# A vision tower's attention: scores and maxima two steps ahead, stacks by group of heads, patches split in other steps

## The chip, the core and the metric

The kernel runs on one core of one Trainium2 chip. The metric is the device time of one execution in microseconds. A core has five engines that run their own instruction streams and meet at semaphores: TensorE (PE in the rows, its weight loads PEld), VectorE (DVE), ScalarE (ACT), GpSimd (POOL) and SyncE (SP), which issues the DMA transfers here.

## The reference

64 images of 224 x 224 go through a patch projection, one attention layer with a residual, and one expert layer with a residual. Cut to what matters:

```python
h = patches(x) @ W.T + b                         # 64 x 196 tokens x 192
xn = layernorm(layernorm(h)) * g + beta          # token-wise, twice
q, k, v = split(xn @ qkv_w.T + qkv_b)            # 12 heads of 16
attn = q @ k.T * 16 ** -0.5                      # 196 x 196 for each head
attn = attn - 0.2 * sum_of_8_neighbours(attn)    # 3 x 3 window, centre left out
attn = softmax(attn - max(attn))
h = h + attn @ v
n = layernorm(h)
score = relu(n @ Wr1.T + br1) @ Wr2.T + br2      # 8 experts, the best 2, softmax weights
h = h + sum over the 2 experts of w_e * (relu(n @ W1[e].T + b1[e]) @ W2[e].T + b2[e])
```

## The kernel before

Two phases follow each other. The change touches the first, the attention phase; the second, the expert phase (router, then 56 tiles of 512 rows), is left as it is.

The attention phase works on pairs of images: 32 pairs, each of four half-image tiles of 98 tokens. A pair has six **steps**: 2 images x 3 groups of 4 heads. A step number within a pair is called k = 0 to 5 here (`kk % STEPS` in the code; `kk` runs over the 12 steps of a body, which is two pairs). The order is written out by hand: each engine has a function `step(body, kk)`, and `run_bodies` (line 137) calls it for a filling, for bodies 0 and 1 written out, for the other bodies in a hardware loop, and for the last body with a drain. Nothing is reordered: an engine that waits in its stream holds all that stands behind it.

What a pair goes through:

1. SyncE loads the patches (`x_buf`, two buffers). ScalarE casts each tile to a 16-bit high part (`high_patches`), GpSimd subtracts to get the low part (`split_patches`), TensorE projects (`project_patches`, 18 matmuls for a tile), VectorE adds the bias (`take_h`) and takes `statistics`; SyncE stores h.
2. GpSimd takes the inverse deviation (`var_eps`, `rstd`) and normalises (`layernorm`, tile `xn`); TensorE transposes (`transpose_xn`); VectorE and ScalarE take the results (`take_xt_a`, `take_xt_b`) and split them into high and low parts (`split_high`, `split_low`).
3. TensorE projects queries and keys in three blocks (`project_qk`); ScalarE evicts them to `padded` (`take_qk`). GpSimd adds the two neighbours (`add_beside`), VectorE adds the centre (`add_tilde`). ScalarE rounds both versions to 16 bits (`take_high_plain`, `take_high_tilde`), VectorE takes what rounding left (`take_low_plain`, `take_low_tilde`). SyncE stores these to DRAM (`store_parts`) and reads them back in stacks of 96 rows (`stack`): one matmul over a stack gives a score with the neighbours already subtracted. Before, 6 transfers of 12 heads each bring a pair's stacks.
4. TensorE projects values (`project_v`); VectorE evicts them (`take_v`).
5. The attention itself, once a step. `scores` (tile `s_bank`, two banks, one for even and one for odd heads) are only for the row maxima (`row_maxima`, `split_maxima` on VectorE). The maxima are transposed (`transpose_max`, into `m_bank`) and copied by ScalarE as extra rows of the query stack (`copy_max_rows`). `scores_less_max` (tile `t_bank`) computes the scores again, transposed, with the maxima subtracted by the matmul. ScalarE takes `exponentials` to `probs`, TensorE multiplies with the values (`mix`), ScalarE copies (`copy_mixed`), TensorE transposes back into `m_bank` (`transpose_back`), VectorE divides (`normalise`).
6. GpSimd adds h (`sum_rows`), VectorE takes statistics (`statistics_n`), GpSimd and ScalarE normalise, split the rows (`high_rows`, `low_rows`) and SyncE stores them for the experts.

In step s TensorE works on the scores of s + 1, the transposed scores of s, the mix of s - 1 and the transposing back of s - 2. The projections of the next pairs lie between, in the functions `before_max` and `after_max`: before and behind the transpose of the maxima. `m_bank` is shared by the transposed maxima and the transposing back, and so `transpose_back` waits for ScalarE's copy of the max rows. In every second pair ScalarE, VectorE and GpSimd also convert a part of the expert weights (`high_part`, `low_part`); in body 0 at kk = 3 SyncE issues the transfers that blank the memory of the expert slots (`blank_memory`).

Of the kernel before, what the change touches and what calls it, by code (L numbers as in the profile page):

```python
# [47 lines left out]
DRAIN = STEPS + 1  # L48
# [88 lines left out]
def run_bodies(eng, step):  # L137

    step(0, -1)
    for body in range(2):  # L140
        for kk in range(BODY_STEPS):
            step(body, kk)
    with eng.Fori(2, BODIES - 1) as body:
        for kk in range(BODY_STEPS):
            step(body, kk)
    for kk in range(BODY_STEPS + DRAIN):
        step(BODIES - 1, kk)


def attention_phase(nc, x_t, w_tok, w_qk_a, w_qk_b, w_v_a, w_v_b, b_tok, b_qk, b_v, ln_cols, row_consts, ident_in,  # L150
# [4 lines left out]
    with ctx:  # L155
# [130 lines left out]
        q_stacked = sem("q_stacked")  # L286
        k_stacked = sem("k_stacked")
# [60 lines left out]
        def patch_uses(u, b):  # L348

            return 1 if isinstance(u, int) and u == 0 else USES[b] * u  # L350
# [10 lines left out]
        def _(sp):  # L361
# [95 lines left out]
            def step(body, kk):  # L457
                k = kk % STEPS
                if kk == -1:
# [5 lines left out]
                    store_h(Pair(0, 0, 0))  # L465
                    for low in range(2):
                        store_parts(Pair(0, 0, 0), low)
                    for low in range(2):
                        stack(Pair(0, 0, 0), low)
                    store_h(Pair(0, 0, 1))  # L470
                elif k == 0:
                    load_x(Pair(body, kk, 2))
                    load_h(Pair(body, kk, -1))
                    store_rows(Pair(body, kk, -2))
                elif k == 1:
                    if kk == 1 and not (isinstance(body, int) and body == 0):
                        store_part(body - 1)
                    elif kk == BODY_STEPS + 1:
                        store_part(body)
                    for low in range(2):  # L480
                        store_parts(Pair(body, kk, 1), low)
                    for low in range(2):
                        stack(Pair(body, kk, 1), low)
                elif k == 3:
                    store_y(Pair(body, kk, -1))
                elif k == 4:
                    store_h(Pair(body, kk, 2))
                if kk == 3 and isinstance(body, int) and body == 0:
# [17 lines left out]
        def _(pe):  # L506
            pe.wait_ge(wtok_split, 2)

            def project_patches(pr, half, c):

                if pr.there:
                    if c == 0:
                        wait(pe, padded_ready, BLOCKS * (pr.u - 1) + (3, 2)[half])
# [4 lines left out]
                    for f in range(PCH):  # L518
# [28 lines left out]
            def project_qk(pr, i):  # L547

                if pr.there:
                    if i == 0:  # L550
                        pe.wait_ge(x_split, 4 * (pr.u + 1))
                    bank, ready = claim(pr, 2 + i)
                    out = bank[:, 0:COLS]
# [6 lines left out]
            def project_v(pr, im, tiles):  # L560

                if pr.there and tiles[0] == 0:
# [3 lines left out]
                    else:  # L566
                        pe.wait_ge(h_ready, 2 * (pr.u + 1) + im + 1)
# [1428 lines left out]
```

## Time and profile before

| | |
|---|---|
| median of three runs | 2195.34 us (2183.92, 2195.34, 2195.45) |
| the profiled execution | 2189.16 us, span 2187.4 us |
| busy share of the span | TensorE 86%, VectorE 67%, ScalarE 58%, GpSimd 53% |
| DMA | 382.56 MB, 175 GB/s on average |
| granted TensorE clock | 0.925 of full speed on average |

The span runs from the first to the last instruction of the profiled execution. Busy shares of a whole span are averages over stages with different limits: the attention phase ends at about 1232 us, and VectorE is busy in it to a much higher share than in the expert phase. In the rows, the bracket at the end of a line gives the idle time of the engine just before the instruction, and what ended it. "issue" stands where the profile names nothing that was waited for.

### The profile page before, as it was taken

How to read it: one execution, taken by the hardware profiler on the slowest of the kernel's cores; microseconds unless marked ns; L12 is line 12 of the kernel's file. 1: busy time of each engine (PE TensorE's matmuls, PEld its weight loads, DVE VectorE, ACT ScalarE, POOL GpSimd, SP SyncE). 2: the span in 40 equal slices, each digit the busy share in tenths (PEclk: the TensorE clock that was granted, in tenths of full speed). 3: DMA queues.
4: the chain of work that ended last, by engine and by line, in shares of the span. 5: the costliest groups of instructions: out<-in, count | busy, mean ns of one | idle time of the engine just before them, and what ended most of it. 6: DMA issues, size and time to landing. Idle time of an engine off the chain costs nothing. (4 is left out here: it accounts for less than half of the span.)

```text
span 2187.4 us, 54001 instructions
## 1 busy us (share of the span) xinstructions
PE 1891.2 (86%) x17949; PEld 1406.2 (64%) x17949; DVE 1461.1 (67%) x4652; ACT 1266.8 (58%) x2469; POOL 1152.0 (53%) x1069
## 2 busy tenths in 40 slices
PE   4758888888888989898888479999999999999991
PEld 3546666666666666666665256777777777777771
DVE  4658888888888888888887345655555555554440
ACT  3557788787878788787877323433434343333330
POOL 3335555555555545555552254666666666654452
PEclk7878999999999999999999559999999999999996
DMA  4564746666574747575664237787877878798876
GB/s 142 144 187 143 202 147 190 168 182 168 173 197 146 215 142 198 161 195 157 183 173 132 65 106 197 186 211 184 206 185 205 190 201 194 190 195 184 180 176 193
DMA packets 356572, 382.56 MB, mean 175 GB/s; under 512 B 138388, under 2 KB 319952, under 8 KB 352144
## 3 DMA queue, kind: packets, MB, share of 16 engines
q1 hardware_dynamic: 314768, 338.64, 55.3%
q0 software_dynamic: 41664, 42.12, 11.1%
q8 instruction: 80, 1.31, 0.2%
q14 instruction: 60, 0.49, 0.1%
HBM read 232.83 MB, written 135.46 MB: 168 GB/s over the span
## 5 line engine op out<-in xcount | busy, mean ns | idle before, releaser
L1838 ACT ACTIVATE mh<-mid_bank 128x512 bf16<-128x512 f32 x336 | 200.8, 598 | 464.0 <-PE mid_bank L1529 349.6
L824 DVE TENSOR_REDUCE row_max<-s_bank 98x2 f32<-98x392 f32 x768 | 396.6, 558 | 97.6 <-PE s_bank L607 94.7
L1750 DVE SCALAR_TENSOR_TENSOR ml<-mid_bank,mh 128x512 bf16<-128x512 f32 x336 | 231.6, 689 | 341.9 <-ACT mh L1838 333.7
L1020 ACT ACTIVATE probs<-t_bank 98x392 f32<-98x392 f32 x768 | 340.6, 498 | 42.1 <-PE t_bank L623 31.1
L1904 POOL DMA_INDIRECT sums<-y_out,tail x168 | 265.1, 1578 | 172.9 <-DVE y_out L1780 95.8
L1543 PE MATMUL y_bank<-wst,mh 128*128 128x192 bf16 x1344 | 330.0, 246 | 8.3 <-DVE y_out L1780 7.5
L1546 PE MATMUL y_bank<-wst,ml 128*128 128x192 bf16 x1344 | 330.1, 246 | 0.0
L1545 PE MATMUL y_bank<-wst,mh 128*128 128x192 bf16 x1344 | 329.8, 245 | 0.0
L623 PE MATMUL t_bank<-q_stack,k_stack 104*98 104x196 f16 x1536 | 248.6, 269 | 40.0 <-ACT probs L1020 25.5
L1193 POOL TENSOR_TENSOR x_lo<-x_buf,x_hi 128x588 f16<-128x588 f32 x128 | 188.7, 1478 | 170.6 <-ACT x_hi L1001 112.8
L1889 POOL DMA_INDIRECT slots<-row_r,spot x196 | 190.7, 973 | 98.0 <-issue 56.7
L623 PEld LDWEIGHTS t_bank<-q_stack,k_stack 104*98 104x98 f16 x1536 | 152.5, 130 | 112.3 <-ACT probs L1020 108.6
L519 PE MATMUL p_bank<-wtok_h,x_hi 128*98 128x192 f16 x768 | 201.7, 263 | 18.2 <-POOL x_lo L1193 18.2
L607 PE MATMUL s_bank<-k_stack,q_stack 96*98 96x196 f16 x1536 | 204.0, 256 | 6.1 <-DVE row_max L824 5.3
L520 PE MATMUL p_bank<-wtok_l,x_hi 128*98 128x192 f16 x768 | 199.7, 260 | 0.0
L521 PE MATMUL p_bank<-wtok_h,x_lo 128*98 128x192 f16 x768 | 198.7, 259 | 0.0
L1037 ACT COPY q_stack<-m_bank 8x784 f16<-8x784 f16 x192 | 154.4, 804 | 66.5 <-PE m_bank L647 63.5
L636 PE MATMUL o_bank<-probs,v_buf 98*32 98x196 f32 x3072 | 171.5, 341 | 18.1 <-ACT probs L1020 18.0
L1201 POOL TENSOR_TENSOR beside<-padded 128x1176 f32<-128x1176 f32 x32 | 68.7, 2146 | 195.3 <-ACT padded L1064 195.3
L607 PEld LDWEIGHTS s_bank<-k_stack,q_stack 96*98 96x98 f16 x1536 | 153.2, 130 | 12.7 <-DVE row_max L824 7.4
L1543 PEld LDWEIGHTS y_bank<-wst,mh 128*128 128x128 bf16 x1344 | 134.3, 100 | 41.1 <-issue 19.5
L1545 PEld LDWEIGHTS y_bank<-wst,mh 128*128 128x128 bf16 x1344 | 131.0, 97 | 19.6
(236 smaller groups left out, 4515.7 us busy)
## 6 DMA issues: line engine op xcount, KB each, us to landing
wst<-packed SPq DMA_DIRECT2D x56, 1584.0 KB
x_buf<-in_x_t SPq DMA_DIRECT2D x32, 1176.0 KB, 9.0
q_stack<-stack_parts SPq DMA_DIRECT2D x96, 294.0 KB, 4.8
k_stack<-stack_parts SPq DMA_DIRECT2D x96, 294.0 KB, 6.7
stack_parts<-qk_hi SPq DMA_DIRECT2D x32, 588.0 KB, 2.9
stack_parts<-qk_lo SPq DMA_DIRECT2D x32, 588.0 KB, 2.8
sums<-h_buf SPq DMA_DIRECT2D x32, 294.0 KB
h_in<-sums SPq DMA_DIRECT2D x32, 294.0 KB
```

Of the source, the lines that this page charges most:

```text
L519: nc.tensor.matmul(out, x_hi[:, f, tokens], wtok_h[:, f, :], start=(f == 0), stop=False)
L520: nc.tensor.matmul(out, x_hi[:, f, tokens], wtok_l[:, f, :], start=False, stop=False)
L607: last = nc.tensor.matmul(s_bank[hh % 2][0:HALF, u, 0:TOKENS], q_stack[st.q][0:PARTS, head, head_cols(st, u)], k_stack[st.q][0:PARTS, head ...
L623: last = nc.tensor.matmul(out, k_stack[st.q][:, head, head_cols(st, v)], q_stack[st.q][:, head, head_cols(st)], start=True, stop=True)
L824: nc.vector.reduce_max(row_max[st.odd][:, :, hh:hh + 1], s_bank[hh % 2][0:HALF, :, 0:TOKENS], AX.X).then_inc(max_ready, 1)
L1020: nc.scalar.activation(probs[st.odd][:, hh], t_bank[hh % 2][0:HALF, :, 0:TOKENS], ACT.Exp).then_inc(probs_ready, 1)
L1543: nc.tensor.matmul(o, mh[n % MID][:, cols], high, start=(c == 0 and j % 2 == 0), stop=False, skip_group_check=True)
L1545: nc.tensor.matmul(o, mh[n % MID][:, cols], low, start=False, stop=False, skip_group_check=True)
L1546: last = nc.tensor.matmul(o, ml[n % MID][:, cols], high, start=False, stop=False, skip_group_check=True)
L1750: nc.vector.scalar_tensor_tensor(ml[n % MID][:], mid_bank[n % MID_PS][:], 0.0, mh[n % MID][:], ALU.max, ALU.subtract).then_inc(ml_ready, 1)
L1838: nc.scalar.activation(mh[n % MID][:], mid_bank[n % MID_PS][:], ACT.Relu).then_inc(mh_ready, 1)
L1904: nc.gpsimd.indirect_dma_start(out=total_rows, out_offset=bass.IndirectOffsetOnAxis(ap=to, axis=0), in_=y_out[q][:, j, :], in_offset=None, ...
```

## The change

- TensorE's `scores` and VectorE's `row_maxima` and `split_maxima` work two steps ahead (`LOOK = 2`), not one; `transpose_max` and `copy_max_rows` stay one step ahead. The filling is four calls of `step` instead of one, the drain is longer by four steps.
- `stack` takes a group of heads: 18 transfers a pair of a third of the size, with semaphores of their own for each group; `scores` waits at the first step of each group of image 0. SyncE issues them in k = 2 and 3, and the patches are loaded three pairs ahead instead of two.
- TensorE's other work is put into `between_heads` (before the last two heads of the second scores) and `after_heads` (behind the transposed maxima): patches in k = 0, 1, 2 instead of 1 and 2, both value projections in k = 3, both transposes of xn at the end of k = 4, query/key behind everything in k = 5.
- VectorE: the second `take_h` in k = 3, both `statistics` at the end of k = 3, both `take_v` in k = 4.
- ScalarE: one patch cast in each of k = 0, 2, 4, 5 (for two or three pairs ahead); `copy_max_rows` directly behind the exponentials; the rows of the second layernorm a pair later.
- GpSimd: one split of patches in each of k = 0, 3, 4, 5, none in k = 1, where it waits for `take_low_plain`.
- The filling interleaves the first two pairs.

```diff
-DRAIN = STEPS + 1
+DRAIN = 2 * STEPS - 1
+LOOK = 2
+FILL = 4
...
-            def stack(pr, low):
+            def stack(pr, low, g):
...
-                        sp.dma_start((q_stack, k_stack)[which][pr.q][32 * r:32 * r + 32], src
-                                     ).then_inc((q_stacked, k_stacked)[which], 16)
+                        sp.dma_start((q_stack, k_stack)[which][pr.q][32 * r:32 * r + 32, HG * g:HG * (g + 1)],
+                                     src[:, :, g]).then_inc((q_stacked, k_stacked)[which][g], 16)
...
                 elif k == 0:
-                    load_x(Pair(body, kk, 2))
+                    load_x(Pair(body, kk, 3))
...
-            def before_max(body, kk):
+            def between_heads(body, kk):
 
                 k = kk % STEPS
-                if k in (1, 2):
-                    project_patches(Pair(body, kk, 2), k - 1, 0)
+                if k in (0, 1):
+                    project_patches(Pair(body, kk, 2), 0, k)
+                elif k == 2:
+                    project_patches(Pair(body, kk, 2), 1, 0, range(PCH // 2, PCH))
                 elif k == 3:
                     project_v(Pair(body, kk, 1), 0, (0, 1))
+
+            def after_heads(body, kk):
+
+                k = kk % STEPS
+                if k == 1:
+                    project_patches(Pair(body, kk, 2), 1, 0, range(PCH // 2))
+                elif k == 2:
+                    project_patches(Pair(body, kk, 2), 1, 1)
+                elif k == 3:
+                    project_v(Pair(body, kk, 1), 1, (0, 1))
                 elif k == 4:
...
                     transpose_xn(Pair(body, kk, 2), 0)
...
                     transpose_xn(Pair(body, kk, 2), 1)
                 elif k == 5:
-                    project_qk(Pair(body, kk, 2), 2)
+                    for i in range(BLOCKS):
+                        project_qk(Pair(body, kk, 2), i)
...
             def step(body, kk):
-                if kk == -1:
+                if kk == -FILL:
                     fill_pipeline()
-                scores(Step(body, kk, 1), (0, 1))
+                scores(Step(body, kk, LOOK), (0, 1))
                 mix(Step(body, kk, -1))
                 transpose_back(Step(body, kk, -2))
                 scores_less_max(Step(body, kk, 0), (0, 1))
-                scores(Step(body, kk, 1), (2, 3))
+                scores(Step(body, kk, LOOK), (2, 3))
+                if kk >= 0:
+                    between_heads(body, kk)
                 scores_less_max(Step(body, kk, 0), (2, 3))
-                if kk >= 0:
-                    before_max(body, kk)
                 transpose_max(Step(body, kk, 1))
                 if kk >= 0:
-                    after_max(body, kk)
+                    after_heads(body, kk)
...
                     elif k == 2:
+                        statistics_n(Pair(body, kk, -1))
+                    elif k == 3:
                         statistics(Pair(body, kk, 2), 0)
-                        statistics_n(Pair(body, kk, -1))
-                        take_h(Pair(body, kk, 2), 1)
-                    elif k == 3:
-                        take_v(Pair(body, kk, 1), 0)
+                        statistics(Pair(body, kk, 2), 1)
```

The order of VectorE around k = 3, first before the change: `h_buf` is the second half of h, `row_max` and `max_parts` the maxima and their split, `stats` and `meanvar` the statistics that GpSimd waits for.

```order
L864 SCALAR_TENSOR_TENSOR h_buf<-p_bank,btok 98x384
L824 TENSOR_REDUCE row_max<-s_bank 98x2 x2
L847 RECIPROCAL recip<-m_bank 98x8
L851 TENSOR_TENSOR att<-m_bank,recip 98x2x64
L872 BN_STATS stats<-h_buf 98x6 x2
L877 MEMSET spacer 98x1
L879 BN_AGGR meanvar<-stats 98x2 x4
L824 TENSOR_REDUCE row_max<-s_bank 98x2 x2
L832 TENSOR_SCALAR max_parts<-row_max 98x2x4
L835 SCALAR_TENSOR_TENSOR max_parts<-row_max,max_parts 98x2x4
L902 TENSOR_TENSOR v_buf<-p_bank,bv 98x24x16
```

And after the change, the same step:

```order
L896 SCALAR_TENSOR_TENSOR h_buf<-p_bank,btok 98x384
L856 TENSOR_REDUCE row_max<-s_bank 98x2 x2
L864 TENSOR_SCALAR max_parts<-row_max 98x2x4
L867 SCALAR_TENSOR_TENSOR max_parts<-row_max,max_parts 98x2x4
L904 BN_STATS stats<-h_buf 98x6 x4
L909 MEMSET spacer 98x1
L911 BN_AGGR meanvar<-stats 98x2 x4
L856 TENSOR_REDUCE row_max<-s_bank 98x2 x2
L879 RECIPROCAL recip<-m_bank 98x8
L883 TENSOR_TENSOR att<-m_bank,recip 98x2x64
L934 TENSOR_TENSOR v_buf<-p_bank,bv 98x24x16 x2
```

The statistics stood ahead of the maxima of heads 2 and 3; now they stand behind them and their split, and values are evicted one step later.

TensorE at the end of k = 4, first before the change (`t_bank` second scores, `s_bank` scores for maxima, `wv` the value projection, `ident,xn` the transposes of xn):

```order
L623 MATMUL t_bank<-q_stack,k_stack 98x196 x4
L607 MATMUL s_bank<-k_stack,q_stack 98x196 x4
L623 MATMUL t_bank<-q_stack,k_stack 98x196 x4
L573 MATMUL p_bank<-wv_ah,x_ah 98x192
L574 MATMUL p_bank<-wv_al,x_ah 98x192
L575 MATMUL p_bank<-wv_ah,x_al 98x192
L576 MATMUL p_bank<-wv_bh,x_b 98x192
L577 MATMUL p_bank<-wv_bl,x_b 98x192
L543 MATMUL p_bank<-ident,xn 128x98 x4
L647 MATMUL m_bank<-ident,max_parts 128x98 x2
L543 MATMUL p_bank<-ident,xn 128x98 x4
```

And after the change, from the transposing back of k = 4 on:

```order
L616 MATMUL m_bank<-ident,mixed 98x128 x2
L650 MATMUL t_bank<-q_stack,k_stack 98x196 x4
L634 MATMUL s_bank<-k_stack,q_stack 98x196 x4
L650 MATMUL t_bank<-q_stack,k_stack 98x196 x4
L674 MATMUL m_bank<-ident,max_parts 128x98 x2
L566 MATMUL p_bank<-ident,xn 128x98 x8
L634 MATMUL s_bank<-k_stack,q_stack 98x196 x4
```

The value projection has left the step, and the eight transposes of xn stand directly behind the transposed maxima, with nothing else between them and the next step's scores.

GpSimd from `beside` (k = 0) to the second layernorm's deviation (k = 2), before the change:

```order
L1201 TENSOR_TENSOR beside<-padded 128x1176
L1193 TENSOR_TENSOR x_lo<-x_buf,x_hi 128x6x98 x4
L1208 TENSOR_TENSOR att<-att,h_in 98x768
L1213 TENSOR_TENSOR var_n<-meanvar_n,eps_n 98x4
L1216 TENSOR_TENSOR rstd_n<-var_n,minus_half 98x4
```

And after the change, from the splits of k = 4 and 5 on:

```order
L1227 TENSOR_TENSOR x_lo<-x_buf,x_hi 128x6x98 x2
L1235 TENSOR_TENSOR beside<-padded 128x1176
L1227 TENSOR_TENSOR x_lo<-x_buf,x_hi 128x6x98
L1242 TENSOR_TENSOR att<-att,h_in 98x768
L1247 TENSOR_TENSOR var_n<-meanvar_n,eps_n 98x4
L1250 TENSOR_TENSOR rstd_n<-var_n,minus_half 98x4
```

One split (`x_lo`) is left behind `beside`; the others went to k = 3, 4 and 5.

## Rows read from the trace of the kernel before

**Rows 1.** Windows: busy us (instructions) by engine, clock, DMA share, GB/s.
```profile
128.50:1161.00 1032.50, 909.48 (x9559) 680.34 (x9560) 870.37 (x2244) 824.95 (x1590) 542.34 (x536) 0.95 0.62 174
```

**Rows 2.** Timeline, GpSimd: start us, us, instruction [idle before, releaser]; once a pair.
```profile
438.15 0.20 POOL L1166 TENSOR_TENSOR var_eps<-meanvar,one_eps 98x4 f32<-98x4 f32 x1 [1.27 <-DVE meanvar L879]
...
473.60 0.20 POOL L1166 TENSOR_TENSOR var_eps<-meanvar,one_eps 98x4 f32<-98x4 f32 x1 [1.00 <-DVE meanvar L879]
...
507.92 0.20 POOL L1166 TENSOR_TENSOR var_eps<-meanvar,one_eps 98x4 f32<-98x4 f32 x1 [1.28 <-DVE meanvar L879]
...
545.00 0.20 POOL L1166 TENSOR_TENSOR var_eps<-meanvar,one_eps 98x4 f32<-98x4 f32 x1 [1.03 <-DVE meanvar L879]
...
616.35 0.20 POOL L1166 TENSOR_TENSOR var_eps<-meanvar,one_eps 98x4 f32<-98x4 f32 x1 [1.00 <-DVE meanvar L879]
...
650.66 0.20 POOL L1166 TENSOR_TENSOR var_eps<-meanvar,one_eps 98x4 f32<-98x4 f32 x1 [1.28 <-DVE meanvar L879]
...
721.43 0.20 POOL L1166 TENSOR_TENSOR var_eps<-meanvar,one_eps 98x4 f32<-98x4 f32 x1 [1.27 <-DVE meanvar L879]
```

**Rows 3.** Waits, 200 to 1050 us: total us, times, longest us.
```profile
DVE row_max L824 <- PE s_bank L607: 65.6, 84, 3.5
...
PE m_bank L647 <- DVE max_parts L835: 43.1, 61, 1.0
...
PE m_bank L589 <- issue: 17.5, 24, 1.0
```

**Rows 4.** Timeline, 619 to 652 us: GpSimd, TensorE, VectorE.
```profile
619.53 2.18 POOL L1183 TENSOR_TENSOR xn<-centred,rstd 98x512 f32<-98x512 f32 x3 [0.17 <-POOL centred L1177]
...
628.94 0.50 PE L607 MATMUL s_bank<-k_stack,q_stack 96*98 96x196 f16 x4
...
639.69 1.44 DVE L931 SCALAR_TENSOR_TENSOR qk_lo<-tilde,tilde_scale,qk_hi 128x1176 f16<-128x1176 f32 x1
...
641.71 1.04 DVE L824 TENSOR_REDUCE row_max<-s_bank 98x2 f32<-98x392 f32 x2 [0.57 <-PE s_bank L607]
...
643.03 0.21 DVE L847 RECIPROCAL recip<-m_bank 98x8 f32<-98x8 f32 x1 [0.28 <-PE m_bank L589]
...
647.61 0.56 DVE L864 SCALAR_TENSOR_TENSOR h_buf<-p_bank,btok 98x384 f32<-98x384 f32 x1 [0.16 <-PE p_bank L521]
...
650.50 1.01 DVE L824 TENSOR_REDUCE row_max<-s_bank 98x2 f32<-98x392 f32 x2
...
651.75 0.17 DVE L835 SCALAR_TENSOR_TENSOR max_parts<-row_max,max_parts 98x8 f16<-98x8 f32 x1
```

**Rows 5.** Source line 921: count, duration ns min/median/max.
```profile
L921 DVE TENSOR_TENSOR qk_lo<-padded,qk_hi x32: 1373/2224/2295, 39.3 to 1167.9; 128x1176 f16<-128x1176 f32 x32
```

**Rows 6.** Windows around falls of the clock, and the router stage.
```profile
666.90:670.40 3.50, 2.02 (x26) 1.02 (x25) 3.41 (x7) 3.45 (x7) 1.69 (x2) 0.93 0.11 42
670.40:677.20 6.80, 6.76 (x45) 6.77 (x46) 5.61 (x9) 5.43 (x10) 4.00 (x3) 0.53 0.22 89
...
520.20:523.60 3.40, 3.40 (x16) 1.86 (x14) 1.13 (x3) 2.27 (x4) 0.00 (x0) 0.57 0.34 127
...
1240.00:1320.00 80.00, 53.01 (x298) 38.87 (x299) 31.16 (x232) 18.69 (x43) 36.36 (x45) 0.50 0.38 118
```

**Rows 7.** SyncE's queue: stack transfers in the timeline, and size, us to landing.
```profile
607.94 1.30 SPq L384 DMA_DIRECT2D q_stack<-stack_parts  x2
...
k_stack<-stack_parts SPq DMA_DIRECT2D x90, 294.0 KB, 6.7
```

**Rows 8.** Timeline of the fill (TensorE, SyncE, ScalarE); groups of the tail, 1161 to 1222.
```profile
73.19 0.89 PE L623 MATMUL t_bank<-q_stack,k_stack 104*98 104x196 f16 x4 [0.56 <-ACT q_stack L1037]
...
117.90 0.43 SPq L366 DMA_DIRECT2D x_buf<-in_x_t  x1
...
127.00 0.68 ACT L1001 CAST x_hi<-x_buf 128x588 f16<-128x588 f32 x1 [17.62 <-DMA x_buf<-in_x_t]
...
L647 PE MATMUL m_bank<-ident,max_parts 98*128 98x98 f16 x22 | 3.0, 218 | 7.1 <-DVE max_parts L835 7.0
```

More of the change, by code:

```diff
@@ L137, in run_bodies @@
 def run_bodies(eng, step):
-    step(0, -1)
+    for kk in range(-FILL, 0):
+        step(0, kk)
     for body in range(2):
@@ L142, in run_bodies @@
             step(body, kk)
-    with eng.Fori(2, BODIES - 1) as body:
+    with eng.Fori(2, BODIES - 2) as body:
         for kk in range(BODY_STEPS):
             step(body, kk)
+    for kk in range(BODY_STEPS):
+        step(BODIES - 2, kk)
     for kk in range(BODY_STEPS + DRAIN):
@@ L599, in scores @@
                 if st.there:
-                    if st.first and heads[0] == 0:
-                        pe.wait_ge(q_stacked, (st.pair + 1) * STACKED)
-                        pe.wait_ge(k_stacked, (st.pair + 1) * STACKED)
+                    if st.image == 0 and heads[0] == 0:
+                        pe.wait_ge(q_stacked[st.group], (st.pair + 1) * STACKED)
+                        pe.wait_ge(k_stacked[st.group], (st.pair + 1) * STACKED)
                     for hh in heads:
@@ new lines, in fill_pipeline @@
+                pe.wait_ge(weights_in, 16 * len(LOADS))
+                pe.wait_ge(consts_set, CONSTS)
+                transpose_xn(first, 0)
+                transpose_xn(first, 1)
+                for c in range(2):
+                    project_patches(second, 0, c)
+                for i in range(BLOCKS):
+                    project_qk(first, i)
+                for c in range(2):
+                    project_patches(second, 1, c)
+                project_v(first, 0, (0, 1))
+                project_v(first, 1, (0, 1))
@@ L936, in fill_pipeline @@
                 first, second = Pair(0, 0, 0), Pair(0, 0, 1)
[L937 to L949 removed]
+                for half in range(2):
+                    take_h(first, half)
+                    statistics(first, half)
+                take_xt_a(first)
+                split_low(first)
+                for half in range(2):
+                    take_h(second, half)
+                    statistics(second, half)
+                add_tilde(first)
+                take_v(first, 0)
+                take_v(first, 1)
+                take_low_plain(first)
+                take_low_tilde(first)
+                take_xt_a(second)
+                split_low(second)
                 set_up_rows()
@@ L1007, in _ @@
             for i in range(2):
+                if i == 1:
+                    for tile in range(TILES):
+                        high_patches(Pair(0, 0, 1), tile)
                 for hh in range(HG):
@@ L1113, in fill_pipeline @@
                     pr = Pair(0, 0, u)
-                    if u == 1:
-                        for tile in range(TILES):
-                            high_patches(pr, tile)
                     take_xt_b(pr)
@@ L1126, in step @@
                 k = kk % STEPS
-                if kk == -1:
+                if kk == -FILL:
                     fill_pipeline()
```

187 lines of the change are left out of this document (91 added, 96 removed).

## The prediction

> **What bounds the kernel now.** I read the stretches first. The steady part of the attention, 1032.5 us, is half of the span; there TensorE is busy 88%, VectorE 84%, ScalarE 80%, GpSimd 53% [rows 1]. No engine is full, so what sets a pair's time is a chain of waits. Second, the pair's period from one instruction that occurs once a pair [rows 2]: 438.15 to 721.43 is 283.3 us for 8 pairs, 35.4 each. An undisturbed pair takes 34.3 (473.60 to 507.92), the one whose steps also convert expert weights 35.5 (438.15 to 473.60), and the one from 507.92 to 545.00 takes 37.1, though of the second kind. Third, the waits [rows 3], for 24 pairs: TensorE stands 43.1 us before the transpose of the maxima and 17.5 before transposing back (nothing named; by the code it waits there for ScalarE's copy of the max rows). That is 2.5 us a pair, and what the change aims at. But VectorE waits 65.6 for scores too, so two engines hand the delay to each other.
>
> The chain of an undisturbed pair, 616.35 to 650.66: GpSimd normalises until xn is ready at 619.53 + 2.18 = 621.71 (5.4 us); TensorE transposes it at once, then query/key, "beside", tilde and the split of the low parts until 639.69 + 1.44 = 641.13 (19.4 us); from there VectorE takes h and its statistics until GpSimd starts at 650.66 (9.5 us, 1.0 of it waits: 0.57, 0.28, 0.16) [rows 2, 4]. Sum 34.3, the measured period. So the loop xn to xn sets the pair, and each edit is priced by what it does to this loop.
>
> **The change, part by part, in the steady state.** (1) Maxima one step earlier: the transpose of the maxima no longer waits, and ScalarE copies the max rows before its other work, not behind it. Both waits go, 2.5 us a pair on TensorE. TensorE was not the loop, though: behind k = 0 and 1 what is late next is VectorE's own row of work (tilde, low plain, two pairs of maxima, low tilde). I value it at nothing beyond the waits of VectorE it removes, counted in (3).
> (2) GpSimd's splits of patches leave step k = 1, where they lay beside VectorE's "low plain" subtraction. That takes 2.22 us in the median but 1.37 at its fastest [rows 5], which is the one that no split overlaps. After the change GpSimd waits for it. It is on the loop: -0.85 us. The Trainium skill (SBUF — State Buffer, "Who interferes with whom") says that a VectorE instruction with two SBUF inputs and a GpSimd one exclude each other; the trace agrees with 2.22 against 1.37, and the value above is the row's.
> (3) Statistics of both halves move behind the maxima of heads 2 and 3 in k = 3. Before, these maxima and their split followed the statistics (650.50 to 651.75 + 0.17, 1.4 us [rows 4]); now they stand ahead of them on VectorE. The 1.0 us of waits in the stretch goes, since TensorE is now a step ahead. Net +0.4 us.
> (4) ScalarE in k = 5: a patch cast (0.68) before the last two exponentials, and the three query/key evictions behind the max rows. The third projection needs the bank of the first, so it waits for that eviction. Worked through with the durations before, k = 5 ends 7.3 us behind xn against 7.2 (621.71 to 628.94 [rows 4]): +0.1; in the odd pair the weight cast makes it +0.7, which before cost 1.2.
> Steady sum without the clock: -0.35 even, about -0.9 odd, mean -0.65 us a pair. Over 29 pairs: -19 us. Bounds: nothing of it (0) to all 2.5 us of TensorE's waits (-73); I stay at the loop.
>
> (5) The new wait. TensorE's xn transposes now stand behind the whole of k = 4, with both value projections already gone to k = 3. Scores of heads 2 and 3 in k = 4 need VectorE's next maxima (1.04 us behind the statistics), so TensorE is through about 1.7 us behind the statistics, and xn comes 5.4 behind them: 3.7 us idle in every pair, where it waited under 0.2. This time is in the loop already. What it does to the clock is not. TensorE's granted clock falls to the lower level (1.2 of 2.4 GHz) after 666.90 to 670.40, in which it waited for 1.5 of 3.5 us; in the router stage, where it idles for a third of 80 us, it stays at 0.50 throughout [rows 6]. The new wait is longer in one piece than what went before the fall at 670.40, so I expect a fall in nearly every pair, covering 3 to 4 us of the transposes, k = 5's scores, mix and back. There TensorE is on the loop: the mix would end at 3.8 instead of 2.2 us behind xn and push ScalarE's exponentials by 1.1 to 1.4. The row of before with a fall at such a place: 507.92 to 545.00 took 37.1, 1.6 over its like, with 0.57 granted at 520.20 [rows 2, 6]; falls with patches beside them cost nothing. Falls cost 35.4 - 34.9 = 0.5 a pair now. I take 1.15 after: +0.6 net, 29 pairs, +17 us. Bounds: 0 granted loss (-16) and 1.6 plus a second stretch, 2.4 a pair (+55).
> The Trainium skill (TensorE: Matmul & The Clock Gate, "HAM oscillation — how this bites in real kernels") says that a kernel whose matmuls come in bursts with waits between is slowed anew after every wait. The rows on the router stage agree; it speaks against this change, and without it the sum would be 17 us lower.
>
> (6) SyncE: 18 stack transfers a pair for 6, same bytes. Issue of one took 0.65 us (two in 1.30 [rows 7]); at that price 3.9 us for the six of group 0, 11.7 in all, of a 35 us period. Median to landing 6.7 us [rows 7]. Group 0 is needed at k = 4 now, not k = 5: low tilde ends at 18.6 in the loop, + 1.1 for the store, + 3.9, + 6.7 = 30.3; TensorE wants it at about 27.5, a microsecond before the statistics end; since xn comes at 33.9 (34.3 - 0.35) and a step's own scores, mix and transposes take about 3, it can take it up to 30.9. Hidden, barely: 0, other end in the rivals. Moved row stores and h stores have whole steps of slack.
>
> **One-time parts.** Fill: the first second-scores start at 73.2 [rows 8]. The second pair's patches, casts and statistics now run inside the first pair's waits. Walking it with the old durations: low tilde of pair 0 is ready 3.3 us later (the second pair's h, statistics and values stand before it), but xn of pair 1 and with it the end of its query/key projections, at about 55, comes 13.4 earlier, group 0's stack lands about then; one more step of scores and maxima is run first. First second-scores at about 60.7: -12.5 (bounds -4 to -16).
> Stall: at 109 ScalarE stands 17.6 us for pair 3's patches, whose load SyncE issues only at 117.9, behind the blank stores, and which lands 9 us later [rows 8]. After the change that load goes out at step 0; the first load behind the blanks is pair 4's, needed two steps later (about 109 in the new frame), issued at 106 to 112: 6 to 12 us of stall remain, and pair 2's stack queues behind it. -7 (bounds 0 to -17.6).
> Tail: the last two pairs have light steps, with 7.0 us of waits of TensorE for the maxima in them [rows 8]; the last pair's rows come 4 steps later but these are empty, except that pair 30's low rows (1.65 us) now stand before pair 31's. -6 + 2 = -4.
>
> **Sum.** -12.5 - 7 - 4 - 19 + 17 = -25.5. The profiled execution took 2189.16 (span 2187.4 + 1.76); it gives 2163.7. The median of the runs shown is 6.2 higher, 2195.34, which would give 2169.8; the three runs lie 11.5 apart, so I take the middle, 2167.
>
> **Rivals.**
> A, the clock does not fall more than now: the 17 us are not paid, 2167 - 17 = 2150. For it: most falls of before lie beside patches and cost nothing; against: the router stage, and the place of this one. With the waits of (1) gaining more than the loop says, down to 2125. Chance 0.25.
> B, no change: falls last twice as long, or cost 1.6 to 2 us a pair, which is +0.85 x 29 = +25: 2192. For it: the 6.8 us stretch at 670.40 [rows 6]. Chance 0.17.
> C, slower: the stack becomes the loop. Group 0's six transfers with the twelve others right behind land later than 30.9 us. Each microsecond beyond costs one a pair; it decides from 0.9 us beyond (25.5 / 29). At 2 us beyond, + 58 - 25.5: about 2225. For it: the 0.6 us of slack above, 9 us landings of patches in the same queue; against: group 0 is a third of the bytes, and is issued first. Chance 0.12.
> D, the edit does not do what it says: TensorE goes on waiting for maxima, since the score banks still allow only two heads ahead, and the loop stays 35.4, with only the one-time parts gained: -23.5, 2169; the same side and nearly the number of my forecast. It shows as waits for row maxima before scores. Chance 0.11.
> Forecast, 0.35: 2167, own range 2148 to 2186.
>
> Faster or slower by under 0.5% (11 us, 2184.4 to 2206.3) is what a measurement cannot tell from no change. Faster: nearly all of A and D, 0.9 of the forecast, 0.15 of B: 0.68. Same: 0.7 of B, 0.1 of the forecast, a fifth of C: 0.18. Slower: the rest, 0.14. The range holds the forecast, most of A, all of B: 2130 to 2204.
>
> **What would show it.** Period of the var_eps instruction: 35.2 even with the clock's loss, 33.9 without (A), over 36 (B, C). TensorE idle 3 to 4 us before the xn transposes each pair, waiting for GpSimd's xn; granted clock of the steady part under 0.95, and below 0.7 right behind that wait. Low plain at 1.4 us. No wait before the transpose of the maxima. C: a wait before the first-step scores for DMA of the stacks. First second-scores at 58 to 66 us. A stall for patches under 12 us near 115. If the transposes don't wait, (5) is wrong, and if low plain stays 2.2, so is (2).

## The result, and the profile after

The changed kernel takes 2277.75 us (median of 4, 2276.83 to 2284.16) against 2194.03 (2183.92 to 2195.45) before: ratio 1.039, 95% interval 1.0375 to 1.0413. It is 84 us slower. The forecast of 2167 and its range failed, and so did the sign.

The span grew from 2187.4 to 2282.1 us, by 94.7. The instruction that occurs once a pair, GpSimd's first on the variance (`var_eps`), splits this into three parts. First its line in both traces (count, min/median/max ns, first and last start), after and then before:

```profile
L1200 POOL TENSOR_TENSOR var_eps<-meanvar,one_eps x32: 200/200/1249, 21.4 to 1235.5; 98x4 f32<-98x4 f32 x32
```
```profile
L1166 POOL TENSOR_TENSOR var_eps<-meanvar,one_eps x32: 198/199/201, 20.0 to 1145.9; 98x4 f32<-98x4 f32 x32
```

Up to the fifth of them the change is ahead: it starts at 179.70 against 184.05, -4.4 us. The 27 periods from there to the last take 39.10 instead of 35.63 us: +94.0. From the last to the end it is 1046.6 against 1041.5: +5.1, which comes from the expert phase, where the program is the same. The loss is the steady pair. The steady stretch of after (columns as in [rows 1]: TensorE matmul, its weight loads, VectorE, ScalarE, GpSimd, clock, DMA share, GB/s):

```profile
130.00:1240.00 1110.00, 916.65 (x9334) 722.63 (x9334) 914.12 (x2214) 809.31 (x1556) 511.53 (x529) 0.85 0.51 159
```

The granted clock is 0.85 where it was 0.95 [rows 1]. VectorE, which was meant to lose waits, has grown in work: 914 us for about the same instructions. Where it grew is in its groups, 200 to 1050 us (busy us, mean ns, idle before): before, then after.

```profile
L832 DVE TENSOR_SCALAR max_parts<-row_max 98x8 f16<-98x8 f32 x143 | 32.2, 225 | 5.0
L835 DVE SCALAR_TENSOR_TENSOR max_parts<-row_max,max_parts 98x8 f16<-98x8 f32 x143 | 24.4, 171 | 4.9
```
```profile
L864 DVE TENSOR_SCALAR max_parts<-row_max 98x8 f16<-98x8 f32 x131 | 89.7, 685 | 5.5
L867 DVE SCALAR_TENSOR_TENSOR max_parts<-row_max,max_parts 98x8 f16<-98x8 f32 x131 | 52.4, 400 | 4.5
```

Two instructions on 98 x 8 numbers went from 0.40 to 1.09 us together, six times a pair: 4.1 us a pair. The timeline of after shows how (start us, us, instruction, [idle before, releaser]), at about the time of [rows 4] (the pair before that one): first k = 4, then k = 1, GpSimd and VectorE.

```profile
615.85 2.18 POOL L1217 TENSOR_TENSOR xn<-centred,rstd 98x512 f32<-98x512 f32 x3 [0.17 <-POOL centred L1211]
```
```profile
615.87 1.62 DVE L864 TENSOR_SCALAR max_parts<-row_max 98x8 f16<-98x8 f32 x1
617.53 0.53 DVE L867 SCALAR_TENSOR_TENSOR max_parts<-row_max,max_parts 98x8 f16<-98x8 f32 x1
...
634.80 1.38 DVE L953 TENSOR_TENSOR qk_lo<-padded,qk_hi 128x1176 f16<-128x1176 f32 x1 [0.44 <-ACT qk_hi L1111]
...
637.16 1.11 DVE L864 TENSOR_SCALAR max_parts<-row_max 98x8 f16<-98x8 f32 x1
```
```profile
636.42 1.83 POOL L1242 TENSOR_TENSOR att<-att,h_in 98x768 f32<-98x768 f32 x1 [2.35 <-DVE qk_lo L953]
```

The split of the maxima ends with GpSimd's instruction: 617.53 + 0.53 = 618.06 against 618.03, and 637.16 + 1.11 = 638.27 against 638.25. So it was held until GpSimd was through, inside its own duration, and no view of waits lists this. Unhindered the two take 0.34 us, 0.17 each. The low plain is down to 1.38 us from 2.2 [rows 5], as forecast; the 0.44 us ahead of it, a wait for ScalarE's rounding, is new.

The waits of after, 200 to 1050 us, that answer to [rows 3]:

```profile
PE p_bank L566 <- POOL xn L1217: 69.3, 22, 3.8
PE s_bank L634 <- DVE row_max L856: 49.1, 33, 1.9
DVE row_max L856 <- PE s_bank L634: 44.9, 51, 2.7
DVE xt_a L917 <- PE p_bank L566: 23.0, 22, 1.6
```

TensorE no longer waits ahead of the transpose of the maxima, but 3.15 us a pair for xn, and 2.2 for row maxima ahead of scores, of which the kernel before has none. Behind the first its clock is down (windows of TensorE: busy, clock, DMA share, GB/s):

```profile
615.40:618.80 3.40, 0.78 (x7) 0.78 0.92 315
618.80:622.20 3.40, 3.40 (x29) 0.50 0.47 136
622.20:625.60 3.40, 3.40 (x24) 0.71 0.00 0
```

For what follows I cut each pair's loop in four, means over the 21 to 25 pairs from 200 to 1080 us, from the timelines of the marks that the prediction used (var_eps, end of xn, start of "beside", end of low tilde); the last column is the mean granted clock in the 4 us that begin 5.4 us behind var_eps, where TensorE starts on xn.

| kernel | var_eps to xn | xn to beside | beside to low tilde | low tilde to var_eps | pair | clock |
|---|---|---|---|---|---|---|
| before | 5.35 | 9.62 | 10.78 | 9.66 | 35.41 | 1.00 |
| after | 5.36 | 10.62 | 11.79 | 11.29 | 39.07 | 0.50 |
| e1 filler | 5.36 | 8.93 | 11.79 | 11.36 | 37.44 | 0.99 |
| e2 sum late | 5.36 | 10.55 | 10.86 | 11.17 | 37.94 | 0.50 |
| e3 stats early | 5.36 | 10.38 | 11.80 | 10.09 | 37.62 | 0.56 |
| e6 patches first | 5.36 | 10.60 | 11.80 | 11.16 | 38.92 | 0.50 |
| e7 (on before) | 5.36 | 9.71 | 11.19 | 9.68 | 35.94 | 1.00 |
| e8 three undone | 5.36 | 10.19 | 10.86 | 10.10 | 36.52 | 0.57 |
| e9 GpSimd order | 5.37 | 9.22 | 10.86 | 8.73 | 34.17 | 0.98 |
| e12 stats, GpSimd order | 5.37 | 10.12 | 11.80 | 8.43 | 35.72 | 0.83 |
| e13 GpSimd order alone | 5.36 | 10.90 | 11.80 | 9.50 | 37.55 | 0.50 |
| e14 (on before) | 5.35 | 10.21 | 10.64 | 11.25 | 37.45 | 0.75 |

The loss has three places: 1.0 behind xn, 1.0 around k = 1, 1.6 on the way to the next var_eps.

Not every microsecond by which VectorE's small instructions grew is on the loop. The six splits of the maxima of a pair take 2.4 us together before, 6.5 in the change, 8.2 in e13 and 4.7 in e9, from the same timelines, and e13 is faster than the change, e9 faster than before. What a collision costs depends on its place.

### The profile page after: what moved, and what is told of

It reads as the page before. It is cut to its first block and busy times, and to the rows that moved or that the text cites. A ratio compares the mean times of both kernels' runs of the same rounds, so it can differ in the third digit from the quotient of the medians.

```text
span 2282.1 us, 54318 instructions
## 1 busy us (share of the span) xinstructions
PE 1925.5 (84%) x17949; PEld 1469.8 (64%) x17949; DVE 1518.4 (67%) x4652; ACT 1270.8 (56%) x2469; POOL 1131.2 (50%) x1069
## 5 line engine op out<-in xcount | busy, mean ns | idle before, releaser
L634 PE MATMUL s_bank<-k_stack,q_stack 96*98 96x196 f16 x1536 | 240.1, 275 | 86.0 <-DVE row_max L856 78.6
L1227 POOL TENSOR_TENSOR x_lo<-x_buf,x_hi 128x588 f16<-128x588 f32 x128 | 167.8, 1314 | 238.1 <-ACT x_hi L1036 174.4
L634 PEld LDWEIGHTS s_bank<-k_stack,q_stack 96*98 96x98 f16 x1536 | 163.3, 138 | 123.7 <-DVE row_max L856 117.6
L650 PE MATMUL t_bank<-q_stack,k_stack 104*98 104x196 f16 x1536 | 229.5, 275 | 14.9 <-ACT probs L1058 13.7
L663 PE MATMUL o_bank<-probs,v_buf 98*32 98x196 f32 x3072 | 191.4, 372 | 16.6 <-ACT probs L1058 15.8
L650 PEld LDWEIGHTS t_bank<-q_stack,k_stack 104*98 104x98 f16 x1536 | 174.8, 140 | 27.8 <-ACT probs L1058 26.1
L566 PE MATMUL p_bank<-ident,xn 98*128 98x98 f32 x256 | 49.4, 373 | 108.5 <-POOL xn L1217 108.5
```

What stands on the lines that cost most here:

```text
L634: last = nc.tensor.matmul(s_bank[hh % 2][0:HALF, u, 0:TOKENS], q_stack[st.q][0:PARTS, head, head_cols(st, u)], k_stack[st.q][0:PARTS, head ...
L650: last = nc.tensor.matmul(out, k_stack[st.q][:, head, head_cols(st, v)], q_stack[st.q][:, head, head_cols(st)], start=True, stop=True)
```

## The experiments

Each was timed together with the kernel before, whose median was 2189 to 2191 us (2194 with the change), so differences to the change of under 5 us tell nothing. Ratios are to the kernel before; the changed kernel's is 1.039.

**e1, filler behind the wait.**
```diff
                     if n == 0:
+                        bank, ready = claim(pr, n)
+                        for _ in range((30 if not isinstance(pr.u, int) or pr.u > 1 else 0)):
+                            nc.tensor.matmul(bank[0:HALF, 0:DIM], x_ah[:, 0:HALF], wv_ah[:], start=True, stop=True)
                         pe.wait_ge(xn_ready, pr.u + 1)
                     bank, ready = claim(pr, n)
```


> The changed kernel with 30 more matmuls of 192 columns (results overwritten) put where TensorE waits for xn at the end of k = 4; they fill about 2.4 of the 3.1 us of the wait and change nothing else. Theory 1 (the clock: the wait for xn makes the granted clock fall over k = 5, and that costs what the loop lost): the low stretch behind the wait goes, xn to end of k = 5 falls from 9.4 back to about 7.3 us, period from 39.1 to about 37, median about 2278 - 2.1 x 27 = 2221. Theory 2 (GpSimd now lies over VectorE's small splits of the maxima, which take 0.69 and 0.40 us in the mean instead of 0.23 and 0.17): period stays within 0.3 of 39.1, median 2270 to 2286.


Measured: 2240.53, ratio 1.0225 (1.0201 to 1.0248). Only "xn to beside" moved, by -1.69 us, with the clock from 0.50 to 0.99. Work that computes nothing makes the kernel 37 us faster: the clock's share is real, 1.6 us a pair, and less than half of the loss.

**e2, row sum behind the low tilde.**
```diff
-                        pool.wait_ge(plain_lo_ready, Pair(body, kk, 1).u + 1)
+                        pool.wait_ge(tilde_lo_ready, Pair(body, kk, 1).u + 1)
                     sum_rows(Pair(body, kk, -1))
```


> The changed kernel, but GpSimd's row sum in k = 1 starts behind VectorE's split of the low tilde and no longer behind the low plain, so that it does not lie over the split of the maxima in k = 1. Theory 2 (port): that split falls from 1.1 to 0.2 us, it is on the loop, period -0.9, median about 2278 - 24 = 2254. Theory 1 (clock only): the 0.9 us is given back as a wait of VectorE or TensorE further on, median 2272 to 2284.


Measured: 2247.90, ratio 1.0251 (1.0228 to 1.0273), -30 us. "Beside to low tilde" fell by 0.93, what the split of the maxima had lost there. It is then as long as before the change, 10.86 against 10.78, although the low plain is 0.8 shorter: VectorE now has two waits in it that the kernel before has not (e2, 200 to 1050 us; total, times, longest):
```profile
DVE qk_lo L953 <- ACT qk_hi L1111: 11.5, 23, 0.6
DVE qk_lo L963 <- issue: 6.4, 23, 0.6
```

**e3, statistics early.**
```diff
                     elif k == 3:
-                        take_h(Pair(body, kk, 2), 1)
+                        statistics(Pair(body, kk, 2), 1)
...
                     elif k == 2:
+                        statistics(Pair(body, kk, 2), 0)
                         statistics_n(Pair(body, kk, -1))
-                    elif k == 3:
-                        statistics(Pair(body, kk, 2), 0)
-                        statistics(Pair(body, kk, 2), 1)
+                        take_h(Pair(body, kk, 2), 1)
```


> The changed kernel with VectorE's take of h and its statistics where they stood before (first half's statistics and the take of the second half at the end of k = 2, second statistics between the maxima of k = 3). Theory 3 (the order sets it: statistics behind the maxima make xn late): xn about 1.4 us earlier, TensorE's wait for it about 1.7 instead of 3.1 us, and if the clock then keeps up another 2: period about 35.7 to 37.7, median 2186 to 2240. Theory 2 (port): the split in k = 4 no longer lies under the normalising, but k = 3's does; period within 0.5 of 39.1 less the 0.3 of order, median 2262 to 2278.


Measured: 2239.65, ratio 1.0225 (1.0199 to 1.0252), -38 us; the wait for xn 1.9 us a pair, the clock still at 0.56. The part of the order came, that of the clock did not.

**e4, one step ahead** (`LOOK = 1`).


> The changed kernel with scores and maxima one step ahead instead of two, all else as changed. Theory A (looking two steps ahead is harmless, the loss is in the other moves): TensorE waits again for the maxima (2 us a pair, not on the loop), median 2268 to 2290. Theory B (two steps ahead itself is the loss: TensorE waits 2.2 us a pair for row maxima before scores of heads 2 and 3, and the fall of the clock in k = 2 comes from it): the wait and the fall in k = 2 go, period 37 to 38, median 2220 to 2250.


Measured: 2391.86, ratio 1.0912 (1.0888 to 1.0937): 114 us slower than the change. Both theories missed. TensorE then waits 180.9 us in 100 transposes of the maxima (200 to 1050 us). Looking two steps ahead is a gain in this order, not the loss.

**e5, value projections apart** (the second image's second tile back in k = 4, VectorE's takes back at the ends of k = 3 and 4).


> The changed kernel with the value projections as before: first image and the first tile of the second in k = 3, its second tile in k = 4, and VectorE takes them at the ends of k = 3 and k = 4. Theory 1 (clock): TensorE has 10 matmuls (0.8 us) and its own pace in k = 4, the wait for xn shrinks from 3.1 to about 2.3 us, the fall stays or goes at random: median 2240 to 2278. Theory 2 (port): VectorE's split of the maxima in k = 4 comes 0.5 us earlier but still under the normalising; nothing on the loop, median 2270 to 2286.


Measured: 2281.81, ratio 1.0428 (1.0395 to 1.0461): as the change. In this order, where TensorE waits for xn anyway, the place of the values costs nothing.

**e6, patches ahead of the scores in k = 2.**
```diff
+                if kk % STEPS == 2 and kk >= 0:
+                    between_heads(body, kk)
                 scores(Step(body, kk, LOOK), (2, 3))
-                if kk >= 0:
+                if kk % STEPS != 2 and kk >= 0:
```


> The changed kernel with, in k = 2 only, the patches that stood behind the scores of heads 2 and 3 put ahead of them, so that TensorE has work while VectorE takes the maxima of heads 0 and 1. If the second fall of the clock (in k = 2, behind waits of 1.6 and 0.8 us for row maxima) is on the loop: it goes or shortens, the later waits of VectorE for scores and of ScalarE for probabilities' input too, period -1 to -1.5, median 2238 to 2250. If it is not: the scores come later for VectorE by the patches' 1.5 us and the period stays or grows, median 2275 to 2310.


Measured: 2273.73, ratio 1.0380 (1.0347 to 1.0414): within 4 us. The fall in k = 2 did go (clock from 12 to 8 us ahead of var_eps: 0.86 in the change, 1.00 here), and so did VectorE's 1.14 us wait for scores in k = 3. VectorE came earlier and met GpSimd (e6, VectorE and then GpSimd):
```profile
643.26 0.83 DVE L866 TENSOR_SCALAR max_parts<-row_max 98x8 f16<-98x8 f32 x1
644.12 1.25 DVE L869 SCALAR_TENSOR_TENSOR max_parts<-row_max,max_parts 98x8 f16<-98x8 f32 x1
```
```profile
642.42 1.64 POOL L1262 TENSOR_TENSOR row<-xn_n,row 98x768 f16<-98x768 f32 x1
644.02 1.32 POOL L1229 TENSOR_TENSOR x_lo<-x_buf,x_hi 128x588 f16<-128x588 f32 x1
```
The split of the maxima takes 2.08 us, where it takes 0.34 unhindered. One cost took the other's place: over all pairs this split takes 2.04 us against 1.21 in the change.

**e7, the kernel before with GpSimd's splits kept off the low plain.**
```diff
                 elif k == 1:
+                    if Pair(body, kk, 1).there:
+                        pool.wait_ge(plain_lo_ready, Pair(body, kk, 1).u + 1)
                     split_patches(Pair(body, kk, 2), (1, 2, 3))
```


> The kernel before with one edit: in k = 1 GpSimd waits for VectorE's split of the low plain before its own three splits of patches. Step (2) of the prediction alone: low plain 1.38 instead of 2.20 us, on the loop, -0.85 a pair, 25 us: about 2167. If GpSimd's splits only move the collision onto VectorE's next SBUF instructions (split of the maxima, low tilde), as in the changed kernel, or patches come late: median 2190 or more.


Measured: 2209.99, ratio 1.0089 (1.0057 to 1.0121): 20 us slower than before, where step (2) had 25 us of gain. VectorE, then GpSimd:
```profile
643.87 1.39 DVE L921 TENSOR_TENSOR qk_lo<-padded,qk_hi 128x1176 f16<-128x1176 f32 x1
646.24 0.51 DVE L832 TENSOR_SCALAR max_parts<-row_max 98x8 f16<-98x8 f32 x1
646.78 1.23 DVE L835 SCALAR_TENSOR_TENSOR max_parts<-row_max,max_parts 98x8 f16<-98x8 f32 x1
```
```profile
645.41 2.57 POOL L1193 TENSOR_TENSOR x_lo<-x_buf,x_hi 128x588 f16<-128x588 f32 x2 [1.95 <-DVE qk_lo L921]
```
The low plain gained 0.8 us, and the two small instructions behind it took 1.74 instead of 0.35, until GpSimd was through at 647.98.

**e8, e2, e3 and e5 together.**


> The changed kernel with three of its parts undone or mended together: the statistics early (e3), the row sum behind the low tilde (e2), the value projections apart (e5). If the three costs are separate pieces of one loop they add: 2278 - 30 - 38 - (0 to 35), about 2175 to 2210. If they hide one another (each only uncovers the next wait): 2220 to 2240, the level of the best single one.


Measured: 2203.12, ratio 1.0053 (1.0033 to 1.0074). The three single effects, -30, -38 and +4, sum to 2214, and the kernel is 11 us below that, so none hides another. But the early statistics were not used in full:
```profile
649.73 1.32 POOL L1228 TENSOR_TENSOR x_lo<-x_buf,x_hi 128x588 f16<-128x588 f32 x1
651.00 0.20 POOL L1201 TENSOR_TENSOR var_eps<-meanvar,one_eps 98x4 f32<-98x4 f32 x1
```
```profile
648.72 0.28 DVE L913 BATCH_NORM_AGGREGATE meanvar<-stats 98x2 f32<-98x6 f32 x3
```
The mean and variance were ready at 649.00; GpSimd was still in the low rows and this split, 2.0 us.

**e9, e8 with GpSimd's own order changed.**
```diff
                 elif k == 2:
+                    low_rows(Pair(body, kk, -2))
                     inverse_deviation_n(Pair(body, kk, -1))
-                    low_rows(Pair(body, kk, -2))
                 elif k == 3:
-                    split_patches(Pair(body, kk, 3), (0,))
...
                         layernorm(Pair(body, kk, 2))
+                    split_patches(Pair(body, kk, 3), (0,))
```


> e8, and GpSimd's order in k = 2 and 3 changed: the low rows ahead of the second normalisation's deviation, the patch split of k = 3 behind the normalising. In e8 the mean and variance are ready at 649.0 us and GpSimd comes at 651.0, since low rows (1.65) and the split (1.32) stand ahead. Theory (in the loop, GpSimd's own order hides what the early statistics gain): the 2.0 us go, less 0.8 for a collision of the low rows with VectorE's split of the maxima; TensorE's wait for xn falls from 2.2 to about 1 us and the clock falls less often: period 36.6 to 34.5 to 35.4, median 2145 to 2170. Rival (VectorE is full in e8, 37.0 to 36.6 us of work and port waits a pair): period within 0.4, 2192 to 2203.


Measured: 2141.91, ratio 0.978 (0.9767 to 0.9800): faster than both kernels, by 49 and 136 us. The clock over 128 to 1100 us is 0.98:
```profile
128.00:1100.00 972.00, 825.28 (x9269) 631.47 (x9269) 856.84 (x2189) 795.61 (x1546) 508.09 (x521) 0.98 0.58 180
```
and the wait for xn (200 to 1050 us) is 0.2 us a pair:
```profile
PE p_bank L566 <- POOL xn L1218: 5.3, 25, 0.3
```

**e10, e9 with 12 fillers.**


> e9 with 12 filler matmuls of 192 columns (about 1 us, results overwritten) ahead of the transposes of xn. If the clock still falls there in e9, this gives back up to 1.6 us a pair as in e1, 2100 to 2145; if e9 has no fall left, nothing or a little slower, within 8 us of e9.


Measured: 2145.59, ratio 0.979 (0.9772 to 0.9806): as e9. With next to no wait left there is no clock to win.

**e11, stacks loaded whole.** The edit: six transfers a pair in k = 2, none by group.


> The changed kernel with the stacks loaded whole as before (6 transfers a pair, not 18), in k = 2. Rival C (the transfers by group are the loop): period falls by 1 or more, under 2250. My reading of the trace after (no instruction waits for a stack; landing 2.5 us): no change, 2270 to 2286; later, if whole stacks land too late for k = 4.


Measured: 2289.35, ratio 1.0442 (1.0415 to 1.0469): 12 us slower than the change. The stacks then land too late for k = 4:
```profile
PE s_bank L634 <- DMA k_stack<-stack_parts: 73.5, 21, 4.5
```

**e12, e3's statistics and e9's GpSimd order, nothing else.**


> The changed kernel with the early statistics of e3 and GpSimd's order of e9, but the row sum in its place of the change and both value projections in k = 3. If the costs are additive pieces: e3's 37.7 less e9's 2.3, period 35.4, median about 2178, and TensorE's wait for xn about as short as in e9 (0.2 us), clock at its upper level. If the value projections in k = 4 are needed to keep TensorE busy: the wait for xn stays over 1 us, clock under 0.95, median 2190 to 2220.


Measured: 2178.69, ratio 0.996 (0.9935 to 0.9976), period 35.8, as the first theory had it: GpSimd's order is worth 61 us on top of e3, as it is on top of e8. The wait for xn is gone (0.1 us a pair), but the clock is not back in full (0.93 over 200 to 1050 us). To e9 it lacks 37 us, of which the row sum gave 30 in e2; whether the place of the values has the rest was not tried.

**e13, e9's GpSimd order alone in the change.**


> The changed kernel with GpSimd's order of e9 alone. With the statistics late, GpSimd is free 1.8 us before them (649.8 against 651.6), so its order can't matter: median 2270 to 2286. If it does matter (the low rows no longer beside the k = 3 maxima split, 0.3 us; or a new collision in k = 2, 0.7): up to 2262 or 2297.


Measured: 2239.09, ratio 1.0230 (1.0206 to 1.0253), -39 us. My reading was wrong. The last piece of the loop fell from 11.29 to 9.50: VectorE's wait for scores in k = 3 is gone (1.14 us, with the fall in k = 2: clock 0.99 there) and nothing lies on its split in k = 3 (0.34 us in every pair). With the late statistics this order is worth 39 us, with the early ones 61 (e12, e9). In k = 4 a new collision took part of it back, the longest of all:
```profile
637.15 3.44 DVE L864 TENSOR_SCALAR max_parts<-row_max 98x8 f16<-98x8 f32 x1
640.63 1.23 DVE L867 SCALAR_TENSOR_TENSOR max_parts<-row_max,max_parts 98x8 f16<-98x8 f32 x1
```
```profile
637.12 2.18 POOL L1217 TENSOR_TENSOR xn<-centred,rstd 98x512 f32<-98x512 f32 x3 [0.17 <-POOL centred L1211]
639.26 2.57 POOL L1227 TENSOR_TENSOR x_lo<-x_buf,x_hi 128x588 f16<-128x588 f32 x2
```

**e14, the kernel before with late statistics.**
```diff
                     elif k == 3:
-                        statistics(Pair(body, kk, 2), 1)
...
                     elif k == 3:
+                        statistics(Pair(body, kk, 2), 1)
                         take_v(Pair(body, kk, 1), 0)
```


> The kernel before with one edit: in k = 3 the second half's statistics stand behind the maxima and their split, as in the change. The prediction's step (3): +0.4 us a pair with 1.0 of waits gone, 2191 + 12 = 2203. If the statistics' delay is paid in full (maxima 1.04 + split 0.35 us = 1.4 a pair) 2191 + 38 = 2229; if TensorE then also waits for xn and its clock falls, about 2240 or more.


Measured: 2254.64, ratio 1.0300 (1.0280 to 1.0320): one moved group of instructions costs 66 us, where the whole change lost 84. The 66 us hold a new wait of TensorE for xn, with the clock at 0.75 behind it, and a longer split of the maxima in k = 4 (1.07 us instead of 0.41):
```profile
641.74 0.56 PE L543 MATMUL p_bank<-ident,xn 98*128 98x98 f32 x4 [1.48 <-POOL xn L1182]
```

## Why the prediction was wrong

The failed steps are (2), (3) and (5): a saving that did not come and brought a collision, waits that did not go, and a price of the clock that was too low. By piece: "beside to low tilde" was forecast 0.85 shorter and became 1.0 longer, "low tilde to var_eps" was forecast +0.4 and became +1.6, and behind xn, forecast +0.7 at most, it became +1.0.

**Step (1)** held as to the waits named: none ahead of the transpose of the maxima. It left out the other side, 2.2 us a pair of TensorE's waits for row maxima ahead of scores, which is the sign that rival D named. By themselves they are no loss: e9 keeps 1.7 us a pair of them, with the clock at 0.98. In k = 2 of the change one of them goes before a fall of the clock.

**Step (2)** failed. The low plain is 1.38 us, but the -0.85 did not reach the loop, for two reasons. The work that GpSimd starts behind it now holds the next VectorE instructions: e7 prices the step alone at +0.5 a pair (period 36.10 against 35.63), and in the change the row sum takes 0.93 (e2). And where nothing collides there (e2, e9) the piece still takes 10.86 us: VectorE waits 0.5 us for ScalarE's rounding ahead of the low plain and 0.3 with nothing named ahead of the low tilde. Which move of the change brought these two waits was not tried. The prediction read a collision as a property of the instruction that it hit, and did not ask what stands behind it. The Trainium skill (SBUF — State Buffer, "Who interferes with whom") says that a VectorE instruction in a mode that takes both pairs of ports and a GpSimd one exclude each other: the one that issues first keeps the shared pair for its whole instruction and the other blocks; it names `tensor_scalar`, which the first instruction of the split is, among those that can run in such a mode. The trace agrees, with 618.06 against 618.03 and 638.27 against 638.25 above.

**Step (3)** set 1.4 us of maxima and split against 1.0 of waits that would go. In the change only 0.3 of 1.2 us of VectorE's waits for TensorE went; 0.7 of the rest is a wait for scores in k = 3, behind the fall of the clock in k = 2, and the split of the maxima that now stands ahead of the statistics takes 1.21 us instead of 0.34. In e13, without this fall and this collision, the waits are gone and the piece takes 9.50 us, less than the 9.66 of before: the netting was right, and what it left out were the clock in k = 2 and GpSimd. The early statistics give 1.4 a pair back in e3. The delay with the waits left in place costs 1.9 in e14 (37.57 against 35.63); the kernel before looks one step ahead, so e14 can't test whether they would go. Of the 1.9, 1.6 are in the last piece and 0.6 behind xn; whether the clock or the longer split in k = 4 sets these 0.6 is not shown.

**Step (5)** had the right mechanism, place and wait (3.7 forecast, 3.15 measured), and too low a price: 1.15 us a pair, where e1 gives back 1.6. It expected 3 to 4 us at the lower level; the clock is at 0.50 for 4 us and 0.60 in the mean over the next 4. The second fall, in k = 2, was not foreseen. One of its readings was wrong too: that falls beside patches cost nothing. The row at 670.40 [rows 6] lies in the pair from 650.66 to 687.11, which took 36.45 us, 1.0 over its like; the shorter ones near this place cost nothing. And its lower bound is 29 x 0.5 = 14.5 us below zero, not 16, on which nothing rests.

**Step (4)** can't be told from the clock's part. **Step (6)** and the rejection of rival C held: no wait for a stack, landing in 2.5 us, and whole stacks (e11) are worse.

**One-time parts.** The fill gained 6.2 us (first second-scores at 67.0 instead of 73.2, half the term of 12.5 and inside its bounds, one above the 58 to 66 that were to show it); ScalarE's stall for patches fell from 17.6 to 8.2, as forecast. Together 19.5 us were expected; only 4.4 are left at the fifth mark: the four periods up to it are 21.0, 47.1, 47.9 and 42.2 us against 33.9, 40.1, 52.1 and 37.9, so that two of them already lose 4 and 7. The tail of the attention held: from the last mark to the last transposing back it is 73.1 us against 76.1, 3 shorter where 4 were forecast. What grew is the expert phase, from its first matmul to the end 949.6 against 943.5, the same program in both; it is 944.4 in e9, 950.8 in e14.

**The sum.** The steady term was -19 + 17 us and came out at +94. No single sum is the account, since one piece changes the worth of another: fillers give 37, the row sum 30, the statistics 38, GpSimd's order 39, and all but the fillers together 136, more than their sum. Every rival was a wait between engines or the clock; none was that VectorE's own instructions get longer, 4.1 us a pair of them, part of it on the loop.

Left open: why the clock doesn't fall in k = 2 in e13, where TensorE idles there as in the change (in one wait of 1.60 us against 1.58, in the pairs around 640 and 625 us). e6 shows that this fall alone is not worth its removal while GpSimd's row and split stand behind it.

## What to carry to other kernels

When GpSimd's work is moved, lay its instructions over VectorE's new order and look at every VectorE instruction whose inputs all lie in SBUF, the smallest ones above all: one of 0.17 us can take 3.4. It costs that much only where the loop stands behind it. Price a move behind other work by the full length of that work unless an experiment shows that the wait it fills was on the loop. And give the critical small chain (statistics, deviation, normalising) the first place on each engine that it passes; e9 did this on two of them and, with the row sum moved, turned +84 us into -49.

## What the runs showed of the hardware

- GpSimd's instructions back to back keep VectorE out across their borders: in e13 a VectorE instruction that started 0.03 us behind GpSimd's sat through three multiplications and one split, 637.15 to 640.59, and the next through the second split. Other VectorE instructions kept their times beside GpSimd's work: statistics of SBUF data (0.61 us for two, at 647.97 in e8), row maxima read from PSUM (0.56 each), and the addition of the bias, with one input in PSUM and one in SBUF (0.55; both in e13).
- Matmuls whose results nobody reads can pay when they fill a wait: 30 of them a pair, 37 us of 2278 (e1), with the clock at 0.99 instead of 0.50.
- The same idle time of TensorE was followed by a fall of the clock in one kernel (change, k = 2: 0.86 in the mean from 12 to 8 us ahead of var_eps) and by none in another (e13: 0.99).
